# Attention scores in two passes over stacked rows, with transfers within SBUF that double q and place k's low part

## The chip, the cores and the metric

The kernel runs on one core of a Trainium2 chip. The metric is the device time in microseconds (us) of one execution. Before the change the median of 3 runs is 690.74 us (690.21 to 692.38).

The engines are called by the names of the profile: PE is TensorE (matmuls), PEld its weight loads, DVE is VectorE, ACT is ScalarE, POOL is GpSimd, SP is SyncE, which only issues transfers.

## The reference

The input x holds 8 x 512 = 4096 tokens of 256 floats. Everything is float32.

```
xn = layernorm(x)
q, k, v = xn Wq^T, xn Wk^T, xn Wv^T            # 16 heads of 16 features
qf, kf = [1, q/2, (q x q)/(4 sqrt 2)], same of k   # so qf.kf = 1 + s/4 + s^2/32,  s = q.k
A = tril(qf kf^T);  y = A v;  z = 1 / (sum over the lower row of A + 1e-12)
attn = (y z) Wo^T
ffn  = top-2 of 8 experts by xn Wg, weights by softmax: (silu(xn W1) * (xn W2)) W3
out  = x + attn + ffn
```

Since 2(1 + s/4 + s^2/32) = (1 + s/4)^2 + 1, the kernel needs only s = q.k of every head, one square per element and a sum.

## The kernel before

The program has an attention phase (up to about 329 us) and an expert phase (71 tiles of 128 rows, to the end). The change touches the attention phase alone.

**Batches and quads.** The outer unit is a batch b of 512 tokens (8 of them); a batch has 4 quads of four heads each, n = 4b + qd, 32 quads in all. k and q are laid out so that a group g (two quads) fills the 128 partitions: partition 32r + 16h + c is feature c of head r in quad 2g + h. One step "c" makes one such array of 128 x 512 in PSUM: ("c", b, 0) is q of group 0, ("c", b, 1) is k of group 0, ("c", b, 2) and ("c", b, 3) are q and k of group 1.

**High and low parts.** A float32 product is made of fp32r matmuls of a high part and a low part. ACT writes the high part (a copy to fp32r), DVE the rest (a subtraction). For q these are `Qh` and `Ql` (128 x 512 each). For k they are `Kh` and `Kl`, and each is written twice, once with the rows of h = 0 alone and once with those of h = 1 (the mask `km` zeroes the other rows), so that a matmul over 32 partitions takes one head's 16 features and 16 zeros.

**The scores.** `scores(n, part)` makes s for four heads at once, four matmuls of 32 partitions side by side (r = 0 to 3). Part 0 has 512 columns, part 1 has 384, part 2 has 256 twice. Each is made of three passes: Kh with Qh, Kh with Ql, Kl with Qh. After each part ACT squares it into T (lines 503, 511 and 517), POOL masks its diagonal (451), and `attend` multiplies by v a quad later (1026). A part's PSUM banks are free for the next part when ACT has squared it.

**Order.** PE's queue in a quad is: scores part 0, attend of the quad before, scores part 1, the steps of `slot_b`, scores part 2, the steps of `slot_c`. The steps fill PE's time while ACT squares. Steps are "x" (transpose of the normalised tokens, L1037), "c" (L1046), "v" (L1055), "C" and "T" (prefix sums of v), "t" (transpose of the attention result, L1075, then the division on DVE, lines 704 to 710), "y" (L1081), "o" (output projection, L1090), "r" (routing). Each takes one of three PSUM banks in turn and has to wait until DVE has released the step three places earlier (`free`). ACT and DVE run their own part of each step in the same order; every engine works its queue strictly in order.

**SP's queue** is one list in program order: loads of x, loads of expert weights into space that the attention phase does not use, and stores of finished rows of `out`. A transfer that waits holds up all behind it.

## Time and profile before

| | us |
|---|---|
| median of 3 runs | 690.74 |
| the profiled execution | 691.0 |
| its span | 689.3 |
| PE busy | 656.5 (95%) |
| DVE busy | 411.7 (60%) |
| ACT busy | 337.8 (49%) |
| POOL busy | 347.0 (50%) |

The span is what the profiler saw on the core; 1.7 us of the execution lie around it. A time that is given as a point, such as 169.94, counts from the start of the span. Matmuls are pipelined, so that rows of PE overlap: how long a piece of PE's work takes is read from start to start. A row can have in brackets how long its engine was idle before it, and which instruction ended that. DMA transfers show two durations: the time of the issuing instruction on its queue (SPq, ACTq), and the time from issue to landing.

### The profile page before, as it was taken

The page shows a single profiled execution, that of the slowest core. Times are in us where ns is not written, and L with a number is a line of the kernel's source. Part 1 is how long each engine was busy: PE and PEld are TensorE (multiplying, and loading weights), DVE is VectorE, ACT ScalarE, POOL GpSimd, SP SyncE. Part 2 cuts the span into 40 slices and gives each one's busy share as a digit, 9 for nine tenths or more (in the row PEclk, how much of TensorE's full clock was granted, in tenths as well). Part 3 has the DMA queues.
Part 4 walks back from the last instruction along what each step waited for, and adds up shares of the span by engine and source line. Part 5 has one row for each costly group of instructions (what it writes and reads, how often), then busy time and mean ns, then how long its engine had stood idle before and what let it go on. Part 6 is the DMA issues. An engine that isn't in the chain of part 4 may idle for free.

```text
span 689.3 us, 17082 instructions
## 1 busy us (share of the span) xinstructions
PE 656.5 (95%) x5863; PEld 511.5 (74%) x5863; DVE 411.7 (60%) x1086; ACT 337.8 (49%) x531; POOL 347.0 (50%) x381
## 2 busy tenths in 40 slices
PE   8899999999999999987899999999999999999994
PEld 6566676666766666653788888888888888888884
DVE  6866776777767666577796544444454545454442
ACT  3667767777768575665573232323232332323231
POOL 3264554546463634456065554545555555545442
PEclk9999999999999999999999999999999999999998
DMA  5220141322211121332853333333333333233332
GB/s 186 76 79 21 49 141 41 101 82 70 67 61 60 58 72 49 110 111 68 298 140 62 64 50 63 53 59 56 56 58 55 61 52 64 49 62 51 64 44 27
DMA packets 29583, 51.50 MB, mean 75 GB/s; under 512 B 4192, under 2 KB 21728, under 8 KB 29504
## 3 DMA queue, kind: packets, MB, share of 16 engines
q0 software_dynamic: 16704, 28.12, 20.7%
q1 hardware_dynamic: 12368, 21.77, 9.7%
q8 instruction: 53, 0.87, 0.5%
q10 hardware_dynamic: 432, 0.53, 0.2%
q14 instruction: 26, 0.21, 0.1%
HBM read 27.72 MB, written 22.68 MB: 73 GB/s over the span
## 4 chain that ended last, share of the span: by engine, by line
PE 85%; DVE 7%; ACT 3%; issue 2%; DMA 1%; POOL 0%; POOLq 0%; SPq 0%; DVEq 0%; ACTq 0%
PE banks L1146 29%; PE banks L1167 15%; PE banks L1026 10%; PE banks L1008 9%; PE banks L1046 7%; PE banks L1155 4%; PE banks L1090 4%; PE banks L1055 3%; PE banks L1135 2%; DVE Kl L724 2%; ACT Kh L533 2%; PE banks L1075 1%; DVE yw L696 1%; DMA wqk_r<-wqk 1%; PE banks L1081 1%
## 5 line engine op out<-in xcount | busy, mean ns | idle before, releaser
L478 POOL DMA_INDIRECT out<-yo,xw x71 | 112.2, 1581 | 155.0 <-DVE yo L966 140.0
L451 POOL TENSOR_SCALAR_AFFINE_SELECT T<-T 128x512 f32<-128x512 f32 x128 | 83.6, 665 | 131.3 <-ACT T L517 45.8
L602 ACT ACTIVATE sTh<-banks 128x512 fp32r<-128x512 f32 x71 | 42.5, 598 | 193.0 <-PE banks L1155 190.0
L1146 PE MATMUL banks<-w12h,xgh 128*128 x284 | 117.8, 415 | 2.3 <-DVE xa L753 1.7
L958 DVE TENSOR_TENSOR sTl<-banks,sTh 128x512 fp32r<-128x512 f32 x71 | 49.1, 691 | 118.2 <-ACT sTh L602 118.2
L1146 PE MATMUL banks<-w12l,xgh 128*128 x284 | 112.1, 395 | 0.0
L1146 PE MATMUL banks<-w12h,xgl 128*128 x284 | 112.1, 395 | 0.0
L467 POOL DMA_INDIRECT xg<-xs_scr,glist x71 | 73.2, 1031 | 22.7 <-issue 19.3
L1026 PE MATMUL banks<-T,vau 128*17 128x512 f32 (+3 forms) x1024 | 77.2, 442 | 0.8 <-POOL T L451 0.8
L503 ACT ACTIVATE T<-banks 128x1024 f32<-128x1024 f32 x64 | 62.1, 1026 | 28.1 <-PE banks L1008 28.0
L442 POOL DMA_INDIRECT xs_scr<-xb,slots x64 | 63.6, 994 | 16.0 <-issue 9.5
L511 ACT ACTIVATE T<-banks 128x768 f32<-128x768 f32 x64 | 48.5, 810 | 34.3 <-PE banks L1008 29.6
L517 ACT ACTIVATE T<-banks 128x768 f32<-128x768 f32 x64 | 48.5, 809 | 28.5 <-PE banks L1008 28.5
L1146 PEld LDWEIGHTS banks<-w12h,xgl 128*128 128x128 f32 x284 | 53.3, 188 | 12.0
L1008 PE MATMUL banks<-Qh,Kh 32*128 32x256 f32 (+2 forms) x512 | 57.1, 397 | 5.4 <-ACT T L517 4.7
L1026 PEld LDWEIGHTS banks<-T,vau 128*17 128x17 f32 x1024 | 26.5, 98 | 47.2 <-issue 39.9
L1146 PEld LDWEIGHTS banks<-w12h,xgh 128*128 128x128 f32 x284 | 53.8, 189 | 9.4 <-issue 2.7
L1146 PEld LDWEIGHTS banks<-w12l,xgh 128*128 128x128 f32 x284 | 53.9, 190 | 6.2
L966 DVE TENSOR_SCALAR yo<-banks,xw 128x256 f32<-128x256 f32 x71 | 34.3, 484 | 39.3 <-PE banks L1167 31.8
L979 DVE TENSOR_TENSOR hs<-banks,hs 128x512 f32<-128x512 f32 x71 | 49.1, 692 | 10.2 <-PE banks L1146 0.8
L1167 PE MATMUL banks<-w3h,sTh 128*128 x284 | 51.1, 302 | 0.8 <-ACT sTh L602 0.8
L1008 PEld LDWEIGHTS banks<-Qh,Kh 32*128 32x128 f32 x512 | 28.1, 182 | 29.6 <-ACT T L503 13.5
(179 smaller groups left out, 1354.3 us busy)
## 6 DMA issues: line engine op xcount, KB each, us to landing
w12r<-w SPq DMA_DIRECT2D x16, 512.0 KB, 4.4
out<-xa SPq DMA_DIRECT2D x16, 256.0 KB
w3r<-w SPq DMA_DIRECT2D x8, 512.0 KB, 5.2
xa<-x SPq DMA_DIRECT2D x7, 512.0 KB, 4.3
xg<-xs_scr,glist POOLq DMA_INDIRECT x71
out<-yo,xw POOLq DMA_INDIRECT x71
xs_scr<-xb,slots POOLq DMA_INDIRECT x64
wqk_r<-wqk SPq DMA_DIRECT2D x1, 512.0 KB, 6.2
```

Of the source, the lines that this page charges most:

```text
L442: e.indirect_dma_start(xs_d, bass.IndirectOffsetOnAxis(slots[:, k, 4 * b + blk:4 * b + blk + 1].bitcast(U32), 0), xb[b % 2][:, blk, :], No ...
L451: e.affine_select(out=v, in_=v, pattern=[[0, 4], [1, P]], compare_op=ALU.is_ge, fill=-1.0, base=0, channel_multiplier=-1).then_inc(s["g_mk ...
L467: e.indirect_dma_start(xg[:, t % GR, :], None, xs_d, bass.IndirectOffsetOnAxis(glist[:, t:t + 1].bitcast(U32), 0)).then_inc(s[f"d_g{t % GR ...
L478: e.indirect_dma_start(out, bass.IndirectOffsetOnAxis(xw[:, t % 4, NE:NE + 1].bitcast(U32), 0), yo[:, t % 2, :], None, compute_op=ALU.add) ...
L503: e.activation(T0[n % 2][:, 2 * h:2 * h + 2, :], banks[:, 2 * h:2 * h + 2, :], ACT.Square, scale=0.25, bias=1.0).then_inc(s["a_s"], 1)
L511: e.activation(T1[:, 2 * h:2 * h + 2, :], banks[:, 2 * h:2 * h + 2, 0:384], ACT.Square, scale=0.25, bias=1.0).then_inc(s["a_s"], 1)
L958: e.tensor_tensor(sTl[:], banks[:, 5, :], sTh[:].bitcast(F32), ALU.subtract).then_inc(s["v_st"], 1)
L979: e.tensor_tensor(hs[:], banks[:, 2 * (t % 2) + 1, :], hs[:], ALU.mult).then_inc(s["v_mu"], 1)
L1008: i = e.matmul(banks[:, r, c0:c0 + w], k[rr, jm * P:(jm + 1) * P], q[rr, 512 - w:512], start=(p == 0), stop=(p == 2))
L1026: i = e.matmul(banks[32 * r:32 * r + HA, 4, 512 - w:512], vau[b % 2][:, jm, 4 * qd + r, :], v[:, r, :], start=(jm == 0), stop=(jm == 2), s ...
L1146: i = e.matmul(banks[:, 2 * (t % 2) + m, :], a[:, k, :], w[:, bass.ds(expert[t] * 4 + (2 * k + m), 1), :], start=(k == 0 and n == 0), stop ...
L1167: i = e.matmul(banks[:, 6 + t % 2, 0:256], a[:, k * P:(k + 1) * P], w[:, bass.ds(expert[t] * 4 + k, 1), :], start=(k == 0 and n == 0), sto ...
```

## The change

`Kh`, `Kl`, `Qh`, `Ql` and `km` go. In their place:

- `K2[:, g, h]`: for head half h, partitions of h hold k's high part and the 16 partitions beside them (of the other half) hold the low part of the same features. ACT writes the high part of all rows into both copies (h = 0 and 1) in one instruction from PSUM; DVE writes the low part of all rows into one buffer `Kt`; then `move_k` copies 16 partitions of `Kt` onto the other half's partitions of `K2`, by four transfers within SBUF (r = 0 to 3) for each h.
- `Q2[g][:, h, p]`: p = 0 is q's high part, p = 1 the low part. ACT and DVE write each for both h at once (128 x 1024 in place of 128 x 512); then `move_q` copies the 16 rows of h, both parts, onto the 16 rows beside them, again four transfers for each h.
- The scores have two passes: K2 with p = 0 and K2 with p = 1. Each sums over 32 partitions, so that (high + low) of k meets high of q, then low of q.
- PE waits for the transfers at part 0 of every quad (`d_q{g}{h}`, `d_k{g}{h}`). DVE waits before it overwrites `Kt` until the transfers from it have landed.
- k and q of group 0 of the next batch are made in `slot_c` of quad 1 and `slot_b` of quad 2 (before: `slot_b` of quads 2 and 3); both "o" steps go to quad 3. In batch 0 all four "v" steps come before the first scores.
- All moves are issued by SP, but for the very first of k, which ACT issues. There are 32 transfers a batch.

```diff
 def slot_b(n):
...
-    else:
-        steps = [("c", b + 1, 3 - qd)]
+    elif qd == 2:
+        steps = [("c", b + 1, 0)]
+    else:
+        steps = [("o", b - 1, 0)] if b else []
 def slot_c(n):
...
-    steps = [("o", b - 1, qd // 2)] if b and qd != 2 else []
     if qd == 3:
-        return steps + [("y", b, 0), ("C", b + 1, 0)]
-    return steps + [("v", b + 1, 2 * qd - 2), ("v", b + 1, 2 * qd - 1)]
+        return ([("o", b - 1, 1)] if b else []) + [("y", b, 0), ("C", b + 1, 0)]
+    return ([("c", b + 1, 1)] if qd == 1 else []) + [("v", b + 1, 2 * qd - 2), ("v", b + 1, 2 * qd - 1)]
...
-FIRST = (("x", 0, 0), ("x", 0, 1), ("c", 0, 1), ("c", 0, 0), ("v", 0, 0), ("v", 0, 1))
+FIRST = (("x", 0, 0), ("x", 0, 1), ("c", 0, 1), ("c", 0, 0), *(("v", 0, i) for i in range(4)))
...
+        def move_q(e, b, g, h):
+            done(e, "c", b, 2 * g)
+            for r in range(4):
+                to, of = 32 * r + 16 * (1 - h), 32 * r + 16 * h
+                e.dma_start(Q2[g][to:to + 16, h].bitcast(F32), Q2[g][of:of + 16, h].bitcast(F32)).then_inc(s[f"d_q{g}{h}"], 16)
+        def move_k(e, b, g, h):
+            done(e, "c", b, 2 * g + 1)
+            for r in range(4):
+                to, of = 32 * r + 16 * (1 - h), 32 * r + 16 * h
+                e.dma_start(K2[to:to + 16, g, h, :].bitcast(F32), Kt[of:of + 16, :].bitcast(F32)).then_inc(s[f"d_k{g}{h}"], 16)
...
# ACT, step "c"
-                    e.activation(Qh[k // 2][:], bank("c", b, k), ACT.Copy).then_inc(s["a_qh"], 1)
-                    for h in range(2):
-                        e.activation(Kh[:, k // 2, h, :], bank("c", b, k), ACT.Copy, scale=km[:, h:h + 1]).then_inc(s["a_kh"], 1)
+                    both = bank("c", b, k).unsqueeze(1).to_broadcast([P, 2, 512])
+                    if k % 2 == 0:
+                        e.activation(Q2[g][:, :, 0, :], both, ACT.Copy).then_inc(s["a_qh"], 1)
+                    else:
+                        e.activation(K2[:, g], both, ACT.Copy).then_inc(s["a_kh"], 1)
...
# DVE, step "c"
-                    release(e.tensor_tensor(Ql[k // 2][:], bank("c", b, k), Qh[k // 2][:].bitcast(F32), ALU.subtract), "c", b, k)
+                    release(e.tensor_tensor(Q2[g][:, :, 1, :], bank("c", b, k).unsqueeze(1).to_broadcast([P, 2, 512]),
+                                            Q2[g][:, :, 0, :].bitcast(F32), ALU.subtract), "c", b, k)
...
-                    for h in range(2):
-                        i = e.scalar_tensor_tensor(Kl[k // 2][:, h, :], bank("c", b, k), km[:, h:h + 1],
-                                                   Kh[:, k // 2, h, :].bitcast(F32), ALU.mult, ALU.subtract)
-                    release(i, "c", b, k)
+                    if 2 * b + g:
+                        for h in range(2):
+                            e.wait_ge(s[f"d_k{1 - g}{h}"], MOVES * (b + g))
+                    release(e.tensor_tensor(Kt[:], bank("c", b, k), K2[:, g, 0, :].bitcast(F32), ALU.subtract), "c", b, k)
...
# PE, scores
-                if part == 0 and h == 0:
-                    done(e, "c", b, 2 * g)
-                    done(e, "c", b, 2 * g + 1)
+                if part == 0:
+                    e.wait_ge(s[f"d_q{g}{h}"], MOVES * (b + 1))
+                    e.wait_ge(s[f"d_k{g}{h}"], MOVES * (b + 1))
...
-                    for p, (k, q) in enumerate(((Kh[:, g, h], Qh[g]), (Kh[:, g, h], Ql[g]), (Kl[g][:, h], Qh[g]))):
+                    for p in range(2):
```

PE's queue in quad 1 of a batch (from scores part 1 on), before the change. L1008 are scores, L1037 "x", L1075 "t", L1090 the output projection "o" of the batch before.

```order
L1008 MATMUL banks<-Qh0_90,Kh_72 128x384 x4
L1008 MATMUL banks<-Ql0_92,Kh_72 128x384 x4
L1008 MATMUL banks<-Qh0_90,Kl0_94 128x384 x4
L1037 MATMUL banks<-ident_49,xb1_135 128x128 x8
L1075 MATMUL banks<-ident_49,yw0_100 128x128 x4
L1008 MATMUL banks<-Qh0_90,Kh_72 128x256 x4
L1008 MATMUL banks<-Ql0_92,Kh_72 128x256 x4
L1008 MATMUL banks<-Qh0_90,Kl0_94 128x256 x4
L1008 MATMUL banks<-Qh0_90,Kh_72 128x256 x4
L1008 MATMUL banks<-Ql0_92,Kh_72 128x256 x4
L1008 MATMUL banks<-Qh0_90,Kl0_94 128x256 x4
L1090 MATMUL banks<-Woh_150,yTh_148 128x256
```

The same place in the changed kernel; L1034 are scores, L1063 "x", L1101 "t", L1072 the step "c" for k of group 0 of the next batch.

```order
L1034 MATMUL banks<-Q20_89,K2_71 128x384 x8
L1063 MATMUL banks<-ident_49,xb1_131 128x128 x8
L1101 MATMUL banks<-ident_49,yw0_95 128x128 x4
L1034 MATMUL banks<-Q20_89,K2_71 128x256 x16
L1072 MATMUL banks<-xTh_139,Wqh_141 128x512
L1072 MATMUL banks<-xTh_139,Wql_142 128x512
L1072 MATMUL banks<-xTl_140,Wqh_141 128x512
```

Twelve score matmuls of 384 columns became eight, 24 of 256 became 16, and the step behind part 2 is "c" where it was "o".

DVE's queue in quad 0 of a batch, from the copy of CT on, before the change; Ql1 is q's low part of group 1, rd and yn the division of step "t", xb1 the normalised tokens of the next batch, Kl1 k's low part.

```order
L740 COPY CT_75<-banks 128x16
L720 TENSOR_TENSOR Ql1_93<-banks,Qh1_91 128x512
L704 TENSOR_SCALAR rd_76<-banks 128x16
L706 RECIPROCAL rd_76<-rd_76 128x16
L710 TENSOR_TENSOR yn_147<-banks,rd_76 128x4x64
L674 TENSOR_SCALAR xb1_135<-xa3_133,mv_142,sm_138 128x256 x4
L724 SCALAR_TENSOR_TENSOR Kl1_95<-banks,km_52,Kh_72 128x512 x2
L749 TENSOR_TENSOR yTl_149<-banks,yTh_148 128x512
```

The same place in the changed kernel:

```order
L769 COPY CT_74<-banks 128x16
L747 TENSOR_TENSOR Q21_90<-banks,Q21_90 128x2x512
L730 TENSOR_SCALAR rd_75<-banks 128x16
L732 RECIPROCAL rd_75<-rd_75 128x16
L736 TENSOR_TENSOR yn_143<-banks,rd_75 128x4x64
L700 TENSOR_SCALAR xb1_131<-xa3_129,mv_138,sm_134 128x256 x4
L755 TENSOR_TENSOR Kt_121<-banks,K2_71 128x512
L778 TENSOR_TENSOR yTl_145<-banks,yTh_144 128x512
```

The order is the same; q's low part has twice the elements, k's low part is one instruction where it was two.

SP's queue from the load of x behind batch 1 to the stores of the batch after, before the change:

```order
L349 DMA xa_130<-x 128x4x256
L322 DMA w12r<-w 128x1024
L319 DMA out<-xa_131 128x2x256 x2
L322 DMA w12r<-w 128x1024
L349 DMA xa_131<-x 128x4x256
```

The same stretch in the changed kernel, where L307 is `move_q` and L314 `move_k`:

```order
L374 DMA xa_126<-x 128x4x256
L307 DMA Q_90<-Q_90 16x1024 x8
L314 DMA K_71<-Kt 16x512 x8
L330 DMA w12r<-w 128x1024
L314 DMA K_71<-Kt 16x512 x8
L307 DMA Q_89<-Q_89 16x1024 x8
L327 DMA out<-xa_127 128x2x256 x2
L330 DMA w12r<-w 128x1024
L374 DMA xa_127<-x 128x4x256
```

Between one load of x and the next stand 32 more transfers: q and k of group 1 of the running batch, then k and q of group 0 of the next.

## Rows read from the trace of the kernel before

**Rows 1.** The page's chain that ended last, by engine and line.

```profile
PE 85%; DVE 7%; ACT 3%; issue 2%; DMA 1%; POOL 0%; POOLq 0%; SPq 0%; DVEq 0%; ACTq 0%
```

**Rows 2.** Busy time by stretch: length, busy (instructions) of each engine, clock, DMA.

```profile
131.80:169.94 38.14, 37.05 (x468) 25.22 (x462) 28.02 (x85) 27.54 (x39) 19.75 (x26) 1.00 0.26 87
```

**Rows 3.** Timeline, PE, batch 4: start us, duration us, then what.

```profile
170.28 0.40 PE L1008 MATMUL banks<-Ql,Kh 32*128 32x512 f32 x4
170.51 0.40 PE L1008 MATMUL banks<-Qh,Kl 32*128 32x512 f32 x4
...
173.40 0.34 PE L1008 MATMUL banks<-Ql,Kh 32*128 32x384 f32 x4
173.57 0.35 PE L1008 MATMUL banks<-Qh,Kl 32*128 32x384 f32 x4
...
176.52 0.29 PE L1008 MATMUL banks<-Ql,Kh 32*128 32x256 f32 x4
176.64 0.29 PE L1008 MATMUL banks<-Qh,Kl 32*128 32x256 f32 x4
```

**Rows 4.** Timeline, quad 0 of batch 4, from step "t" to step "y".

```profile
175.41 0.60 PE L1075 MATMUL banks<-ident,yw 128*128 128x128 f32 x4
175.62 0.60 ACT L528 ACTIVATE Qh<-banks 128x512 fp32r<-128x512 f32 x1 [0.15 <-PE banks L1046]
...
176.25 0.69 DVE L720 TENSOR_TENSOR Ql<-banks,Qh 128x512 fp32r<-128x512 f32 x1 [0.92 <-ACT Qh L528]
...
177.34 0.42 DVE L710 TENSOR_TENSOR yn<-banks,rd 128x256 f32<-128x256 f32 x1
...
178.35 0.60 PE L1081 MATMUL banks<-ident,yn 128*128 128x128 f32 x4
```

**Rows 5.** Timeline, quad 1 of batch 4, the chain on DVE.

```profile
182.30 0.69 DVE L696 TENSOR_TENSOR yw<-banks,CT 128x512 f32<-128x512 f32 x1 [0.44 <-PE banks L1026]
...
185.34 1.29 DVE L717 TENSOR_TENSOR xTl<-banks,xTh 128x512 fp32r<-128x512 f32 x2
...
186.08 0.39 PE L1090 MATMUL banks<-Woh,yTh 128*128 128x256 f32 x1 [0.55 <-DVE xTl L717]
```

**Rows 6.** Timeline, quad 2 of batch 4, the high and low part of k; quad 2 of batch 3.

```profile
194.78 1.27 ACT L533 ACTIVATE Kh<-banks,km 128x512 fp32r<-128x512 f32 x2
196.08 1.41 DVE L724 SCALAR_TENSOR_TENSOR Kl<-banks,km,Kh 128x512 fp32r<-128x512 f32 x2 [2.40 <-ACT Kh L533]
...
159.41 0.39 PE L1055 MATMUL banks<-Wvh,xTh 128*128 128x264 f32 x1 [0.53 <-DVE Kl L724]
```

**Rows 7.** By line and form, 100 to 300 us: instructions of 1024 elements.

```profile
L503 ACT ACTIVATE T<-banks 128x1024 f32<-128x1024 f32 x42 | 40.8, 1027 | 17.7 <-PE banks L1008 17.7
L683 DVE TENSOR_TENSOR w12l<-w12r,w12h 128x1024 fp32r<-128x1024 f32 x6 | 7.3, 1220 | 0.1
```

**Rows 8.** Issue of single transfers on SP's queue; then landing times, by issues.

```profile
7.91 0.33 SPq L308 DMA_DIRECT2D wo_r<-wo  x1
...
301.19 0.51 SPq L322 DMA_DIRECT2D w12r<-w  x1
...
wv_r<-wv ACTq DMA_DIRECT2D x1, 264.0 KB, 6.4
...
wo_r<-wo SPq DMA_DIRECT2D x1, 256.0 KB, 2.6
```

**Rows 9.** Timeline, the start: k's high part, scores parts 0 and 1.

```profile
12.12 1.27 ACT L533 ACTIVATE Kh<-banks,km 128x512 fp32r<-128x512 f32 x2 [1.29 <-PE banks L1046]
...
15.82 0.51 PE L1008 MATMUL banks<-Qh,Kh 32*128 32x512 f32 x4
...
20.03 0.45 PE L1008 MATMUL banks<-Qh,Kh 32*128 32x384 f32 x4
```

**Rows 10.** Timeline, a wait of PE in batch 7; the stretch behind it.

```profile
311.66 0.50 PE L1008 MATMUL banks<-Qh,Kh 32*128 32x512 f32 x2 [1.77 <-ACT T L517]
...
312.00:316.00 4.00, 3.80 (x28) 1.20 (x30) 3.77 (x5) 2.25 (x3) 3.38 (x3) 0.68 0.00 0
```

More of the change, by code:

```diff
@@ L41, in slot_a @@
 def slot_a(n):
[L43 removed]
+    return [("C", 0, 0)] if n == 0 else []
 def slot_b(n):
@@ L194, in build @@
         rg = [w3_hi(2 * g, 2 * g + 2) for g in range(2)]
[L195 to L197 removed]
+        Q2 = [rg[g].take(f"Q2{g}", 2048, F32R, (2, 2, 512)) for g in range(2)]
         T0 = [w3_lo(2 * u, 2 * u + 2).take(f"T0{u}", 2048, F32, (4, 512)) for u in range(2)]
@@ L325, in load_w3 @@
                 e.dma_start(W3r[:, rows(n), :], w3[:, rows(n), :]).then_inc(s[f"d_t{n}"], 16)
+            move_q(e, 0, 0, 0)
+            move_k(e, 0, 0, 1)
+            move_q(e, 0, 0, 1)
+            for b in (2, 3):
+                e.dma_start(xa[b][:], xin[b]).then_inc(s[f"d_x{b}"], 16)
+            e.wait_ge(s["c_z"], 2)
+            e.dma_start(xs_d[SPARE:SPARE + P, :], zero[:]).then_inc(s["d_z"], 16)
+            e.dma_start(out[NTOK:NTOK + P, :], zero[:, 0:D]).then_inc(s["d_z"], 16)
             for b in range(NBATCH):
+                for h in range(2):
+                    move_q(e, b, 1, h)
+                for h in range(2):
+                    move_k(e, b, 1, h)
                 if b == 0:
@@ L334, in sync_program @@
                     load_w12(11)
+                if b < LAST:
+                    for h in range(2):
+                        move_k(e, b + 1, 0, h)
+                    for h in range(2):
+                        move_q(e, b + 1, 0, h)
                 if b:
```

39 lines of the change are left out of this document (15 added, 24 removed).

## The prediction

> **What bounds the kernel now.** I read the chain of waits first: PE stands in 85% of it, DVE in 7%, ACT in 3% [rows 1]. So the time is PE's queue, read start to start, plus the few places at which PE waits for another engine. The busy time by stretch says how much room there is: one batch takes 38.14 us, of which PE is busy 37.05, DVE 28.02, ACT 27.54 and POOL 19.75, at a granted clock of 1.00, which is the level of 2.4 GHz [rows 2]. PE thus waits about 1.1 us a batch, and the reader is to see in the timeline that this is two waits: 0.55 us in quad 1, behind DVE's xTl, and 0.53 us in quad 2, behind DVE's Kl [rows 5, 6]. Everything else in a batch is PE's own work, with DVE and ACT close behind it. That decides how I count: what PE saves is worth its whole time only where the next thing that PE needs was made with slack to spare.
>
> **What goes from PE.** One of three passes. From the second pass to the third of the same part takes 170.51 - 170.28 = 0.23 us at 512 columns, 173.57 - 173.40 = 0.17 at 384 and 176.64 - 176.52 = 0.12 at 256 [rows 3]. A quad has one part of 512, one of 384 and two jobs of 256: 0.23 + 0.17 + 2 x 0.12 = 0.64 us. Over 32 quads that is 20.5 us, and it is the most that this edit can give. The passes that stay have the same partitions and columns as before, so I give them their old length. The steps that change places are of one length: "c" is six matmuls of 512 columns, 6 x 0.23 = 1.4 us, and "o" twelve of 256, 12 x 0.12 = 1.4 us. The move itself costs PE nothing.
>
> **What is added on ACT and DVE.** ACT's q copy goes from 0.60 us [rows 4] to 1024 elements, for which an ACT row says 1.03 [rows 7]: +0.43. DVE's low part of q goes from 0.69 [rows 4] to 1024 elements, 1.22 [rows 7]: +0.53. For k, ACT goes from 1.27 for two copies [rows 6] to one of 1024, 1.03: -0.24; DVE from 1.41 for two to one of 512 elements, 0.69: -0.72. Reading a bank twice through a broadcast is shown by no row; I take the length of a plain instruction with as many elements. Its ends are 0.69 (nothing for the second copy) and 2 x 0.69 = 1.38. Sums per batch hardly change (ACT +0.4, DVE -0.4). What matters is which of them PE waits for.
>
> **Quad 0 of a batch.** Take the start of "t" on PE (175.41) as zero [rows 4]. Before, ACT's q copy starts at 0.2, Ql at 0.84, the division that follows it on DVE ends at 1.93 + 0.42 = 2.35, and "y", which needs it, starts at 2.94. There is 0.59 us of slack. Now the division is late by 0.43 + 0.53 = 0.96 and "y" wants to start 0.24 earlier (part 2 is shorter). The wait is 0.96 + 0.24 - 0.59 = 0.61 us. Quad 0 keeps 0.64 - 0.61 = 0.03 us.
>
> **Quad 1.** From the end of attend DVE runs a fixed chain: copy of yw at 182.30, routing, xTl at 185.34, and PE's step behind part 2 starts at 186.08 after 0.55 us of idle [rows 5]. The step is now "c" in place of "o", but it takes the same bank, released by the same xTl. What PE saves between attend and this point (0.17 + 0.24) only makes the wait longer, 0.96 in place of 0.55. Quad 1 keeps 0.23.
>
> **Quad 2.** PE's second "v" waits 0.53 us for Kl [rows 6]. In its place comes q's chain: 1.03 + 1.22 = 2.25 us where Kh and Kl took 1.27 + 1.41 = 2.68. It starts when ACT has squared part 1, which moves with PE. So this point moves 0.43 us relative to part 1 (PE alone would have been ready 0.24 + 0.53 sooner), and the quad keeps 0.23 + 0.17 + 0.43 = 0.83.
>
> **Quad 3.** No k or q is made in it; the rows show no wait here, and the two "o" steps need only banks long released: 0.64. Sum of a batch: 0.03 + 0.23 + 0.83 + 0.64 = 1.73 us of the 2.56 that PE saves. The rest turns into waits for DVE.
>
> **The transfers.** This is the part that no row shows. SP issues 16 in a row in quad 0 and 1 (q, then k of group 1). Single issues on SP take 0.33 to 0.51 us; landing from issue takes 2.6 us for the smallest load on SP and up to 6.4 us for the slowest row [rows 8]. I take 0.43 and 2.6. The tightest waiter is DVE, which must not write `Kt` for k of the next batch until those of this one have landed. On the old time scale, with the gains above: Q2's low part ends near 177.5, so 16 issues end at 177.5 + 6.9 = 184.4 and the last lands at 187.0. `Kt` is wanted behind "c" of quad 1: 186.08 - 0.20 + 1.45 for the step, 1.1 for ACT's copy, 188.4. That leaves 1.4 us. With the largest issue, 0.51, it is 188.3: just in time. With 6.4 us of landing it is 2.4 us late, but there DVE has some 2 us of other work before PE needs anything of it again, so the first 2 us cost little. PE's own waits (`d_q`, `d_k`) have more room: k of group 1, first half, lands by about 186 and is needed near 189; group 0 has all of quad 3. Cost taken: nothing, hidden by that room; its ends are nothing and, with every transfer at the slow row, about 0.5 us a batch.
>
> The Trainium skill, "SBUF — State Buffer", section "Door 1: The DMA port swizzle", says that a transfer's rate depends on how many of 16 ports its partitions reach, in clusters of four partitions. By it, 16 partitions reach 4 ports, an estimate of 435/16 x 4 = 109 GB/s, so 64 KB of q would take 0.6 us against an issue of 0.43. By that rule the last k transfer lands some 1.4 us later and eats the room just worked out, without a cost; no row here has so narrow a transfer.
>
> **The start.** In batch 0 the transfers are in the open. ACT: k copy from 12.12 to 13.15 [rows 9], q copy to 14.2, DVE's low part to 15.5; SP issues four (1.7 us), and the last, issued at about 16.8, lands at 19.4. Part 0 of the scores starts then and not at 15.82. Part 1 stood at 20.03 [rows 9], because "v" steps and "C" came between; the "v" steps now fill the wait, and part 1 has to wait for ACT's two squares only: 19.4 + 0.67 + 2.05 = 22.1, 2.1 us later. The shorter parts 1 and 2 give back 0.4. Start: +1.5 to +1.7; I take 1.5. The other three quads of batch 0 save 1.7 as in every batch. If the gap lets PE's clock fall to 1.2 GHz, about 1 us more: after a wait of 1.77 us in batch 7 the granted clock of the next 4 us is 0.68, a mix of the two levels [rows 10].
>
> **Batch 7.** It has little to fill PE, which then waits for ACT's squares (1.77 us in one place [rows 10]). Those follow from the scores, so a shorter pass moves them too: 3 x 0.64, and 0.03 for its quad 0: 2.0. The expert phase is not touched.
>
> **Sum.** +1.5 - 1.7 (batch 0) - 6 x 1.73 = 10.4 (batches 1 to 6) - 2.0 (batch 7) = -12.6 us. The profiled execution took 691.0: 678.4. The median of the runs, 690.74, lies 0.3 below it: 678.
>
> **Rivals.**
> - *The whole saving arrives.* DVE's longer q part finds slack (a broadcast read that is cheaper, the end at 0.69), so that quads 0 and 2 have no wait. For: DVE and ACT are busy under 75% of a batch [rows 2]. Against: the 0.59 us of slack in quad 0 and the chain in quad 1, which no edit shortens. With only the chain of quad 1 left: 7 x (2.56 - 0.41) + 2.6 (batch 7) - 1.5 = 16.1; with all of it 20.5 - 1.5 = 19. Time 672 to 675.
> - *Slower: SP's queue gates DVE.* If a narrow transfer takes SP c us to issue and L to land, `Kt` is written at 177.5 + 16c + L at the earliest, against 188.4 + 2 that DVE can absorb. At c = 0.43, L may be 6.0. At c = 0.9 and L = 2.6 it is 194.5, 4.1 us late, 7 times: 29 us against 12.6 gained, 707. It loses more than the change gains (1.8 us a batch) from c of about 0.76 on, half again the largest row of SP. For: no row of this size, no transfer within SBUF. Against: the issue of 256 KB takes 0.33 and that of 512 KB 0.51 [rows 8], so a small one should not take more.
> - *Half of it.* ACT in quad 0 (q copy, squares, k copy, "y", squares without a gap) and DVE's later `Kt` and "v" work push further waits of 0.5 to 1 us into two quads of each batch: 7 us less, 685 or so. For: both engines' gaps in quads 0 and 1 are under 1 us once stretches shrink.
> - *The new order does not carry its part* (the moved steps bring a bank wait of their own of 1.7 us or more a batch): within 2 us of 691.
>
> **Chances.** Forecast (674 to 682) 0.52; whole saving 0.18; half of it 0.17; no gain 0.05; slower 0.08. A run of this kernel can tell 0.3% (2 us) from no change. Faster by over 0.3%: 0.87; within 0.3%: 0.04; slower: 0.09. The range 671 to 687 leaves out the last two cases and the ends of the others.
>
> **What would show it right or wrong.** In the profile after: score passes start to start 0.23, 0.17 and 0.12 as before, two of each; DVE's low part of q 1.22 and ACT's copy 1.03; a batch of 36.4 us. PE idle before "y" of quad 0 by 0.6, before "c" of quad 1 by 1.0, before the second "v" of quad 2 by about 0.2 to 0.6, and none before scores part 0 behind a DMA, but for the first. The first scores at about 19.4. I am wrong if scores or `Kt` wait for DMA in every batch, if issues on SP take over 0.7 us, or if quad 0 has no wait before "y".

## The result and the profile after

The changed kernel took 687.07 us, the median of its 19 runs (683.07 to 690.13), against 690.74 us before (688.42 to 693.58, measured beside it). The medians lie 3.7 us apart, the means (686.5 and 691.2) 4.7. The ratio over all runs is 0.9929, with a 95% interval of 0.9916 to 0.9942. So it is faster, by 0.5 to 0.7%. The forecast was 678.0 with a range of 671 to 687: the direction is right, but only about a third of the 12.7 us arrived, and the time lies just outside the range. The profiled execution of the changed kernel is the slowest of the 19, 690.1 us with a span of 688.4, against 691.0 and 689.3 before. Part of what follows is that execution's own, and I say where.

The way to read such a pair is to take the same landmarks on PE in both traces and subtract. Landmarks here are the first matmul of part 0 of the scores of a quad, the first matmul of the experts, and the first transpose of `hs` of the first and the last tile.

| stretch on PE | before, us | after, us | change | forecast |
|---|---|---|---|---|
| 0 to quad 1 | 26.50 | 29.83 | +3.3 | +1.5 |
| quads 1 to 3 of batch 0 | 28.40 | 26.64 | -1.8 | -1.7 |
| batches 1 to 4 | 153.21 | 150.97 | -2.2 | -6.9 |
| batches 5 and 6 | 76.27 | 73.43 | -2.8 | -3.5 |
| batch 7 to the first expert matmul | 44.38 | 42.91 | -1.5 | -2.0 |
| from there to the first tile's transposes | 9.26 | 10.95 | +1.7 | 0 |
| to the last tile's transposes | 339.76 | 342.08 | +2.3 | 0 |
| rest of the span | 11.5 | 11.6 | +0.1 | 0 |

The last column adds up to the forecast of -12.6, the one before it to -0.9. Attention alone is 5.0 us shorter at its end; the experts hand 4.1 of that back.

The chain that ended last, by engine (answers to [rows 1]):

```profile
PE 72%; DVE 11%; issue 5%; DMA 5%; ACT 3%; SPq 2%; POOL 1%; POOLq 0%; DVEq 0%
```

PE fell from 85% to 72% of it. Busy time by stretch, batch 4 and batch 6 (columns as in [rows 2]):

```profile
169.78:207.44 37.66, 34.75 (x405) 22.53 (x400) 28.51 (x83) 28.27 (x37) 19.80 (x27) 1.00 0.46 115
244.15:280.87 36.72, 34.54 (x404) 22.52 (x398) 22.42 (x69) 26.37 (x35) 17.91 (x26) 1.00 0.44 107
```

PE's busy time dropped from 37.05 to 34.75, which is 2.3 of the 2.56 us that the pass was worth. The length of a batch dropped by 0.5 in the first row and by 1.4 in the second. The rest is idle time of PE: 2.9 and 2.2 us a batch, where [rows 2] had 1.1. To see where it stands, cut a batch into its quads. Batch 5 before, four quads (length, then PE's busy time first):

```profile
208.11:217.15 9.04, 9.04 (x112) 5.97 (x107) 6.81 (x20) 6.56 (x11) 3.82 (x6) 1.00 0.32 104
217.15:227.34 10.19, 9.63 (x121) 6.91 (x118) 8.35 (x24) 7.14 (x11) 5.15 (x9) 1.00 0.05 16
227.34:236.63 9.29, 8.76 (x103) 5.68 (x103) 5.27 (x19) 6.19 (x8) 4.65 (x6) 1.00 0.21 75
236.63:246.23 9.60, 9.60 (x139) 6.65 (x138) 6.37 (x23) 5.75 (x9) 5.47 (x7) 1.00 0.13 47
```

The same batch after, and ahead of it quad 3 of batch 4:

```profile
197.59:207.44 9.85, 9.10 (x130) 6.29 (x130) 8.47 (x25) 5.78 (x8) 6.80 (x9) 1.00 0.54 125
207.44:216.62 9.18, 8.58 (x98) 5.29 (x92) 6.84 (x18) 7.43 (x12) 3.70 (x6) 1.00 0.38 109
216.62:226.78 10.16, 8.93 (x98) 5.87 (x94) 7.12 (x22) 7.47 (x10) 4.28 (x8) 1.00 0.44 88
226.78:235.23 8.45, 8.11 (x88) 5.08 (x87) 5.99 (x21) 5.99 (x7) 5.03 (x7) 1.00 0.28 82
235.23:244.15 8.92, 8.92 (x130) 6.29 (x130) 5.87 (x23) 5.47 (x7) 6.06 (x9) 1.00 0.60 136
```

Quad 0 is longer than before by 0.14 and quad 1 as long as before, although PE works 0.5 and 0.7 us less in them. Quad 2 gains 0.84, quad 3 gains 0.68. And quad 3 of batch 4 is 0.93 longer than that of batch 5.

The two waits that were forecast are there. Quad 0 of batch 4 (answers to [rows 4]; time, duration, then what):

```profile
174.84 0.60 PE L1101 MATMUL banks<-ident,yw 128*128 128x128 f32 x4
175.04 1.03 ACT L556 ACTIVATE Q<-banks 128x1024 fp32r<-128x1024 f32 x1
176.10 1.23 DVE L747 TENSOR_TENSOR Q<-banks,Q 128x1024 fp32r<-128x1024 f32 x1 [1.17 <-ACT Q L556]
177.72 0.42 DVE L736 TENSOR_TENSOR yn<-banks,rd 128x256 f32<-128x256 f32 x1
...
178.29 0.63 PE L1107 MATMUL banks<-ident,yn 128*128 128x128 f32 x4 [0.59 <-DVE yn L736]
```

ACT's copy takes 1.03, DVE's part 1.23, and PE stands 0.59 us ahead of "y". These are the three numbers of the forecast, within 0.02. But from the start of "t" to the start of "y" it takes 178.29 - 174.84 = 3.45 us. The forecast had 2.94 + 0.96 - 0.59 = 3.31: it let "y" start when yn ends (177.72 + 0.42 = 178.14), and PE starts it 0.15 us later. Quad 1 (answers to [rows 5]):

```profile
182.04 0.69 DVE L722 TENSOR_TENSOR yw<-banks,CT 128x512 f32<-128x512 f32 x1 [0.98 <-PE banks L1052]
...
184.22 0.63 POOL L476 TENSOR_SCALAR_AFFINE_SELECT T<-T 128x512 f32<-128x512 f32 x1 [1.78 <-ACT T L536]
184.30 0.60 DVE L825 TENSOR_TENSOR eq<-oh,rk 128x32 f32<-128x32 f32 x1
...
185.36 1.29 DVE L743 TENSOR_TENSOR xTl<-banks,xTh 128x512 fp32r<-128x512 f32 x2
...
186.10 0.50 PE L1072 MATMUL banks<-xTh,Wqh 128*128 128x512 f32 x1 [1.18 <-DVE xTl L743]
```

From the copy of yw to xTl DVE needs 3.32 us here and 3.04 in [rows 5], so PE waits 1.18 and not 0.96. In between, one small instruction of DVE with two inputs in SBUF starts 0.08 us behind a mask of POOL and takes 0.60 us; before, it took 0.19 and started ahead of the mask.

What was not forecast stands in quad 3 of batch 4 (DVE's and POOL's rows of quads 2 and 3):

```profile
197.25 1.21 POOL L476 TENSOR_SCALAR_AFFINE_SELECT T<-T 128x512 f32<-128x512 f32 x2
197.36 2.18 DVE L709 TENSOR_TENSOR w12l<-w12r,w12h 128x1024 fp32r<-128x1024 f32 x1
...
202.69 0.69 DVE L722 TENSOR_TENSOR yw<-banks,CT 128x512 f32<-128x512 f32 x1
...
203.53 0.63 PE L1101 MATMUL banks<-ident,yw 128*128 128x128 f32 x4 [0.75 <-DVE yw L722]
```

DVE's split of an expert weight takes 2.18 us, and 1.22 on average before [rows 7]. It starts 0.11 us behind a pair of POOL's masks. Before, it started first, and then POOL paid (1.85 us for a pair that takes 1.21 here):

```profile
198.23 1.22 DVE L683 TENSOR_TENSOR w12l<-w12r,w12h 128x1024 fp32r<-128x1024 f32 x1
198.69 1.85 POOL L451 TENSOR_SCALAR_AFFINE_SELECT T<-T 128x512 f32<-128x512 f32 x2 [0.98 <-ACT T L517]
```

So in these rows whichever of the two starts first runs at its own length and the other waits for it. The Trainium skill, "SBUF — State Buffer", section "SBUF: two separate sides", says so of such a pair: a DVE instruction with two SBUF inputs and a GpSimd one that reads SBUF take an exclusive lock. The rows agree: the one that came second lost 0.96 us (DVE) or 0.64 us (POOL).

The transfers (answers to [rows 8]; issue min/median/max in ns, then landing, then who waited):

```profile
L307 SPq DMA_DIRECT2D Q<-Q x128: 507/589/1843, 15.9 to 292.8; - x128
...
DMA to landing us min/median/max: 2.2/2.4/3.6
...
L314 SPq DMA_DIRECT2D K<-Kt x124: 507/589/1669, 18.7 to 297.8; - x124
...
  DVE Kt L755: 17.5, 7
```

An issue costs 0.59 us in the median, not 0.43, though it moves 32 or 64 KB; landing is 2.4 for those of q. DVE waits for Kt's release seven times, 2.5 us on the average.

The start (answers to [rows 9]), and then the granted clock of three stretches (length, busy times, third from last the clock):

```profile
15.95 2.73 SPq L307 DMA_DIRECT2D Q<-Q  x4
20.55 1.23 PE L1034 MATMUL banks<-Q,K 32*128 32x512 f32 x8 [2.91 <-DMA Q<-Q]
```

```profile
20.00:28.00 8.00, 7.17 (x71) 4.64 (x71) 5.28 (x22) 4.21 (x7) 2.31 (x3) 0.57 0.45 75
300.00:312.00 12.00, 10.47 (x117) 5.28 (x109) 10.80 (x26) 6.27 (x8) 9.00 (x11) 0.86 0.54 185
320.00:328.00 8.00, 6.67 (x25) 5.36 (x26) 3.54 (x8) 3.19 (x5) 2.84 (x3) 0.57 0.75 260
```

PE is at 1.2 GHz in three places: for about 7, 3 and 7 us (a granted clock of 0.57 over 8 us means (1 - 0.57) x 2 x 8 = 6.9 us at half clock, and so on). The kernel before had one such place, of about 3 us, between 313 and 317 us, the one that [rows 10] shows in part.

Last, the scatter of the experts' results, on POOL and in DVE's copy that waits for it:

```profile
341.38 1.63 POOL L503 DMA_INDIRECT out<-yo,xw  x1 [17.35 <-DVE yo L992]
348.94 2.08 POOL L503 DMA_INDIRECT out<-yo,xw  x1 [3.62 <-DMA out<-yo,xw]
...
354.34 0.17 DVE L980 COPY xw<-xg 128x16 f32<-128x16 f32 x1 [1.74 <-DMA out<-yo,xw]
```

Each scatter waits until the one before it has landed. The first took 6.8 us to land, beside the last loads of weights, and the tiles from the sixth to the twelfth came late, together by 2.3 us. This is the +2.3 of the table. I take it for this execution's own: in eleven of the twelve traces below the same stretch takes 339.7 to 340.0 us, as before, and it is longer only with twice as many transfers (341.0), where the first scatter took 7.4 us to land. Without it the profiled execution would be 3.2 us faster than before, which fits the 3.7 of the medians.

### The profile page after: what moved, and what is told of

It is laid out like the page before. It is cut to its first block, busy times and chain, and to the rows that moved or that the text cites. A ratio compares the mean times of both kernels' runs of the same rounds, so it can differ in the third digit from the quotient of the medians.

```text
span 688.4 us, 16296 instructions
## 1 busy us (share of the span) xinstructions
PE 643.7 (94%) x5351; PEld 494.4 (72%) x5351; DVE 411.1 (60%) x1067; ACT 342.6 (50%) x515; POOL 346.5 (50%) x381
## 3 DMA queue, kind: packets, MB, share of 16 engines
q1 hardware_dynamic: 20432, 34.24, 20.3%
## 4 chain that ended last, share of the span: by engine, by line
PE 72%; DVE 11%; issue 5%; DMA 5%; ACT 3%; SPq 2%; POOL 1%; POOLq 0%; DVEq 0%
PE banks L1172 27%; PE banks L1193 14%; PE banks L1052 8%; PE banks L1034 5%; PE banks L1072 4%; PE banks L1181 4%; PE banks L1116 3%; DVE Q L747 3%; DMA out<-yo,xw 2%; PE banks L1161 2%; ACT Q L556 2%; PE banks L1081 2%; DVE yw L722 1%; PE banks L1107 1%; SPq L307 1%
## 5 line engine op out<-in xcount | busy, mean ns | idle before, releaser
L503 POOL DMA_INDIRECT out<-yo,xw x71 | 114.1, 1607 | 159.3 <-DVE yo L992 85.7
L476 POOL TENSOR_SCALAR_AFFINE_SELECT T<-T 128x512 f32<-128x512 f32 x128 | 79.8, 635 | 121.1 <-ACT T L528 51.7
L492 POOL DMA_INDIRECT xg<-xs_scr,glist x71 | 71.1, 1001 | 24.2 <-issue 23.0
L1034 PE MATMUL banks<-Q,K 32*128 32x256 f32 (+2 forms) x1024 | 71.7, 363 | 5.9 <-DMA Q<-Q 2.9
L467 POOL DMA_INDIRECT xs_scr<-xb,slots x64 | 67.2, 1050 | 18.4 <-issue 9.6
L1034 PEld LDWEIGHTS banks<-Q,K 32*128 32x128 f32 x1024 | 38.6, 185 | 30.2 <-ACT T L528 13.9
```

Source lines behind the costliest of these rows:

```text
L467: e.indirect_dma_start(xs_d, bass.IndirectOffsetOnAxis(slots[:, k, 4 * b + blk:4 * b + blk + 1].bitcast(U32), 0), xb[b % 2][:, blk, :], No ...
L476: e.affine_select(out=v, in_=v, pattern=[[0, 4], [1, P]], compare_op=ALU.is_ge, fill=-1.0, base=0, channel_multiplier=-1).then_inc(s["g_mk ...
L492: e.indirect_dma_start(xg[:, t % GR, :], None, xs_d, bass.IndirectOffsetOnAxis(glist[:, t:t + 1].bitcast(U32), 0)).then_inc(s[f"d_g{t % GR ...
L503: e.indirect_dma_start(out, bass.IndirectOffsetOnAxis(xw[:, t % 4, NE:NE + 1].bitcast(U32), 0), yo[:, t % 2, :], None, compute_op=ALU.add) ...
L1034: i = e.matmul(banks[:, r, c0:c0 + w], K2[rr, g, h, jm * P:(jm + 1) * P], Q2[g][rr, h, p, 512 - w:512], start=(p == 0), stop=(p == 1))
```

## The experiments

Each was run beside the kernel before on the same chip (its medians 691.6 to 692.2 us there). A ratio is against it. The changed kernel itself stands at 0.9929. Ratios of single edits have intervals about 0.004 wide, so they seldom tell such an edit from the changed kernel; the traces do, though each shows one execution. Where an edit is not shown, or is shown in part, "..." marks it or the text says so.

**Without the transfers.** It leaves out the copies within SBUF and the waits for them, so one of the two row halves holds the wrong part of q or k.

```diff
-            done(e, "c", b, 2 * g)
+            return
             for r in range(4):
...
# the same in move_k; DVE's wait for d_k goes; PE, scores
-                    e.wait_ge(s[f"d_q{g}{h}"], MOVES * (b + 1))
-                    e.wait_ge(s[f"d_k{g}{h}"], MOVES * (b + 1))
+                    done(e, "c", b, 2 * g)
+                    done(e, "c", b, 2 * g + 1)
```

> Leaves out the transfers within SBUF and the waits for them: the rows of q and k beside each other then both hold the high copy or the low part as written, so the result is not attention's; every instruction of PE, ACT and DVE stays. Theory A (the transfers cost only the gap at the start; what the batches lack lies on DVE and POOL): first scores near 17 instead of 20.55, quad 1 starts at about 26.5 instead of 29.83, batches 1 to 4 stay at 37.6 us and batches 5 and 6 at 36.7; the expert phase takes back a part, so 683.5 to 685.5 us against 687.1 of the changed kernel. Rival B (the issues of 0.59 us on SP and the late gate on Kt are what the batches lack): batches 1 to 6 at 36.4 as forecast, another 5 to 6 us, so 678 to 680.

Measured: 688.1 us, ratio 0.9950 (0.9931 to 0.9969). First scores at 17.64, but batch 1 starts at 57.21, later than the 56.47 with transfers. Without the gap ahead of the first scores PE waits 2.2 us for DVE's CT and 1.4 for ACT's squares between 25 and 29 us, and the clock is halved from 27 to 34. Batches 1 to 6 take 38.03, 37.68, 37.66, 37.66, 36.72 and 36.71 us, equal to the changed kernel's within 0.03.

So in a steady batch 32 transfers cost nothing. Of theory A the batches are right. The forecast of 683.5 to 685.5 failed: quad 1 starts at 28.87 and not at 26.5, because the waits come back behind the first scores, and the slow stretch comes all the same.

**The new order alone**, three passes and no transfers, the tables of slots taken from the changed kernel.

```diff
+    elif qd == 2:
+        steps = [("c", b + 1, 0)]
     else:
-        steps = [("c", b + 1, 3 - qd)]
+        steps = [("o", b - 1, 0)] if b else []
...
```

> The kernel before with three passes and no transfers, but with the new order of the steps (v steps ahead of the first scores, c in quad 2 and 1, o in quad 3). Theory A (the moved steps cost PE nothing): 690.7 within 1 us, batches of 38.1 us. Rival B (the new order brings waits of its own, above all DVE's later work in quads 2 and 3): batches of 38.6 us or more, 693 to 696 us, which would account for most of what the whole change lacks.

Measured: 689.25 us, ratio 0.9968 (0.9955 to 0.9981), batches 2 to 6 of 37.24 to 37.27. Both theories failed. Its batch 5 by quads:

```profile
206.23:215.28 9.05, 9.05 (x114) 5.98 (x108) 6.72 (x20) 6.42 (x11) 2.92 (x5) 1.00 0.35 104
215.28:225.41 10.13, 9.57 (x114) 6.59 (x110) 7.20 (x22) 8.41 (x13) 5.07 (x9) 1.00 0.05 16
225.41:233.91 8.50, 8.50 (x103) 5.63 (x102) 6.48 (x22) 5.56 (x7) 4.65 (x6) 1.00 0.14 50
233.91:243.48 9.57, 9.57 (x145) 6.90 (x145) 6.17 (x22) 5.47 (x7) 6.40 (x10) 1.00 0.22 74
```

The order alone brings nearly the whole gain of quad 2, 0.79 of 0.84 us. From these rows to the changed kernel's, the missing pass with all that comes with it (longer q parts, transfers) changes quads 0 to 3 by +0.13, +0.03, -0.05 and -0.65: it pays only in quad 3, the one quad in which PE waits for nobody. What two passes would bring in the old order with the transfers left out was not run, so the two shares hold for this sequence of steps.

**The weight split moved.**

```diff
+                if qd == 2 and (b, qd) in W12_LOW_WITH:
+                    w12_low(W12_LOW_WITH[b, qd])      # end of before_b, no longer in after_b
```

> The changed kernel with one DVE instruction moved: w12_low of quad 2 goes ahead of the slot with c, away from POOL's pair of masks. Theory A (DVE's w12l of 1.22 us is stretched to 2.18 by POOL's masks in quad 2 of batches 1 to 4, and PE pays 0.74 us for it in quad 3): w12l back to 1.22, no wait for yw before t in quad 3, batches 1 to 4 at 36.9 instead of 37.65, 3 us at the first expert matmul, 684 to 686 us at the end since the expert phase gives some back. Rival B (the quad 3 wait comes from the length of DVE's queue, not from the overlap): wait stays 0.5 us or more, or moves to the second v of quad 2 (low part of q later by up to 1.2 us): 687 to 690.

Measured: 686.03 us, ratio 0.9920 (0.9901 to 0.9939). Batches 2 to 6 take 36.73 to 36.75 each, as theory A has it; the time is at the upper end of its 684 to 686. The moved split in the timeline:

```profile
190.78 1.22 DVE L709 TENSOR_TENSOR w12l<-w12r,w12h 128x1024 fp32r<-128x1024 f32 x1
```

and quad 3 of batch 4 by stretch, no longer with idle time of PE:

```profile
194.82:203.74 8.92, 8.92 (x129) 6.28 (x128) 6.04 (x23) 5.78 (x8) 6.24 (x9) 1.00 0.61 138
```

The overlap with POOL's masks is the cause of the 0.93 us in batches 1 to 4. The next run shows it a second time, without an edit of that place. The first expert matmul comes 2.1 us sooner than in the changed kernel: 3.7 are won in batches 1 to 4, and 1.5 lost again from batch 7 to that matmul, where this trace has half clock from 295 to 299 and from 316 to 326 us.

**PE filled ahead of the first scores.**

```diff
+            for _ in range(26):
+                e.transpose(banks[:, 0, 0:P], ident[:], ident[:])
             for n in range(NQ):
                 scores(n, 0)
```

> The changed kernel with 26 transposes into bank 0 ahead of the first scores, which keep PE busy through the wait for the first transfers; nothing that is computed changes. Theory A (the 2.9 us of idle drop the granted clock to half until 26.8 us): the clock stays at 1.0 from 20 to 27 us, quad 1 starts 1.5 to 2 us sooner (28.0 instead of 29.83), 685 to 686 us. Rival B (the clock falls whatever PE does there, or the start is set by ACT's squares and DVE): quad 1 stays at 29.8, 687 us.

Measured: 686.4 us, ratio 0.9934 (0.9912 to 0.9957). Theory A failed: quad 1 starts at 31.60 and not at 28.0. The gap of 2.9 us is 1.0 us now, but the first scores come at 21.51, since SP's first four issues took 3.77 us where they took 2.73, and the clock still falls, and stays low from about 24 to 30.5 us: behind the first scores PE waits again, for ACT's squares, 0.5 us twice.

In this trace DVE's split started ahead of the masks in quad 2 of batches 2 and 3, and behind them in batches 1 and 4:

```profile
85.24 2.18 DVE L709 TENSOR_TENSOR w12l<-w12r,w12h 128x1024 fp32r<-128x1024 f32 x1
123.05 1.22 DVE L709 TENSOR_TENSOR w12l<-w12r,w12h 128x1024 fp32r<-128x1024 f32 x1
```

Quad 3 takes 8.93 and 9.15 us in batches 2 and 3, and 9.84 to 9.86 in batches 1 and 4 as in the changed kernel (though quad 2 of batch 2 is 0.57 longer here). So the order of starts is what decides, in one and the same execution.

**PE filled in all thin stretches.**

```diff
+            spin(0, 26)
             for n in range(NQ):
+                if n > NQ - 4:
+                    e.wait_ge(s["v_yw"], n - 1)
+                    spin(4, 9)
...
+                if n == 0:
+                    e.wait_ge(s["c_b4"], 1)
+                    spin(4, 8)
...
             attend(NQ - 1)
+            e.wait_ge(s["a_s"], 6 * NQ)
+            spin(2, 8)
             step("t", LAST, 3)
+            spin(2, 6)
```

> The changed kernel with idle stretches of PE filled by transposes of a constant whose result nobody reads: 26 ahead of the first scores, 8 ahead of part 1 of quad 0, 9 ahead of the scores of quads 29, 30 and 31, 14 around the last t. Theory B (a part of the gain goes to half clock: 7 us at the start, 5 in batch 7, 7 at the first expert, against one stretch of 6 in the kernel before; each is set off by a stretch in which PE mostly waits): granted clock 1.00 in at least two of the three places, first tile's transposes 3 to 4 us sooner (331 instead of 334.7), 683 to 684.5 us. Rival (the clock falls whatever fills the gaps, as it did at the start with 26 transposes alone): the same three stretches, 687 us.

Measured: 685.19 us, ratio 0.9909 (0.9892 to 0.9926); the first tile at 330.98 where the changed kernel has 334.73. The same three stretches as above:

```profile
20.00:28.00 8.00, 6.98 (x90) 4.88 (x89) 4.95 (x26) 4.69 (x8) 2.32 (x3) 1.00 0.46 80
300.00:312.00 12.00, 10.36 (x137) 6.53 (x129) 11.35 (x25) 6.71 (x9) 9.01 (x11) 1.00 0.49 179
320.00:328.00 8.00, 7.02 (x45) 5.82 (x43) 4.72 (x10) 5.13 (x8) 1.72 (x2) 1.00 0.91 323
```

The clock is 2.4 GHz in all three, and no microsecond from 8 us to the first tiles shows half clock. PE still waits here in places, up to 1.6 us for yw in batch 7, without a fall. Batch 1 starts at 55.14 instead of 56.47, although the first scores come 1.4 us later (21.92), and from the first expert matmul to the first tile it takes 9.24 instead of 10.95, as before (9.26). Theory B holds for the clock: the slow stretches cost at least 1.3 us at the start and 1.7 at the experts. Its time, 683 to 684.5, is missed by 0.7 us; the profiled execution is the fastest of the six and the one with the highest clock.

The stretch at the experts can be read in other traces as well. It takes 9.25 us where the clock does not fall behind the first expert matmul (the gather's run below), 10.19 where it stays low for 2.9 us (26 transposes alone), 10.95 for 3.7 (the changed kernel) and 12.00 for 6.1 (the second buffer, below).

**DVE's order in quads 0, 1 and 2.**

```diff
+    if qd == 0 and n:
+        return [("T", b, 0), ("t", (n - 1) // 4, (n - 1) % 4), ("c", b, 2)]
...
-                    place_rows(b)      # before_b, quad 1
...
+                elif qd == 1 and b < LAST:
+                    place_rows(b)      # after_b
```

(and the moved weight split of above)

> The changed kernel with three orders changed, nothing added: in quad 0 the step T and t go ahead of c; in quad 1 DVE makes xTl ahead of the slots of the routing; in quad 2 w12_low goes ahead of DVE's part of q. Theory A (the passes removed in quads 0 and 1 turn into waits for DVE, 0.60 before y and 1.18 before c, and are to be had once DVE's order gives them): quad 0 8.6 instead of 9.17, quad 1 9.4 instead of 10.19, batches of 35.4 us instead of 37.65 and 36.71, 12 us less at the first expert matmul, 675 to 678 us. Rival (DVE or ACT has no room, the waits reappear a quad later): batches 36.5 or more, 685 us.

Measured: 681.51 us, ratio 0.9853 (0.9831 to 0.9874); batches 37.82, 36.79, 37.01, 36.59, 35.71, 37.25. The time misses theory A's 675 to 678. Quads 0 and 1 came out nearly as it says, 8.67 and 9.52; but in five of six batches quad 2 takes 9.5 to 10.2. DVE's row behind quad 1 of batch 4:

```profile
187.70 0.69 DVE L757 TENSOR_TENSOR Kt<-banks,K 128x512 fp32r<-128x512 f32 x1 [3.02 <-DMA K<-Kt]
```

and quad 2 by stretch, PE idle for 1.1 us of it:

```profile
185.37:194.84 9.47, 8.41 (x88) 4.91 (x87) 7.04 (x22) 7.36 (x9) 8.70 (x10) 1.00 0.34 97
```

Here the rival is right as well: a wait comes back a quad later. Its candidate is Kt's release, which now comes 3 us late.

**The gather behind the masks.**

```diff
-                    if n == NQ - 1 and m == 1:
+                    if n == NQ - 1 and m == 3:
```

> The changed kernel with POOL's first gather behind the last two masks instead of ahead of them. Theory C (the gather waits 2.7 us for the last rows sent, and the masks behind it hold PE for 2.1 us at the end of attention): attend of quad 31 waits under 0.6 us, the gather itself starts no later (316.6), the first expert matmul 1.5 to 2 us sooner (322 instead of 323.8); at the end 1 to 2 us less, 685 to 686. Rival (the landing of the gather sets the first expert): attend is sooner, but the expert's first matmul stays at 323.8 and the time at 687.

Measured: 685.25 us, ratio 0.9908 (0.9884 to 0.9932), which overlaps the changed kernel's. From quad 31's first scores to the first expert matmul it takes 15.0 us; the changed kernel takes 18.1 and the kernel before 17.1. In the changed kernel PE's waits of that stretch are led by this one (us in total, times, longest):

```profile
PE banks L1052 <- POOL T L476: 2.3, 2, 2.1
```

It is gone here, and the clock does not fall at the experts. The gather starts at 318.26, which is 10.6 us after quad 31's start, where it was 10.9. Of theory C the wait holds. Its size is less sure: with the gather in its old place the stretch also takes only 16.4 us in the run with 26 transposes and 16.7 in that with a second buffer, so that 1.4 to 3.1 us are the gather's. And the first expert matmul is at 322.75 and not at 322, since quad 31 itself starts 2.0 us later here, behind half clock from 300 to 303 us.

**The old order with two passes and transfers.** The tables of slots are those of the kernel before.

> The changed kernel (two passes, transfers) with the order of steps of the kernel before. In it DVE's low part of q for the next quad 0 ends about 2 us before that quad's first scores, and 4 issues and a landing of some 2.4 us come behind it. Theory A (the new order is what hides the transfers, and brings 0.9 us a batch by itself): PE waits 2 to 4 us for a transfer ahead of the scores of quad 0 in every batch, batches of 39 to 41 us, 700 to 715 us. Rival (the transfers find room in either order): batches of 37.5 to 38, 687 to 690 us.

Measured: 718.97 us, ratio 1.0397 (1.0366 to 1.0429); batches of 40.8 to 42.6. Theory A's mechanism holds, its 700 to 715 us are too low. PE's waits in one batch of it (146.88 to 187.67):

```profile
PE banks L1033 <- DMA Q<-Q: 5.5, 2, 2.8
```

So the new order is what hides the transfers. "Made a quad sooner" is no extra of the change but its condition: without it, the kernel would have been 27 us slower than before.

**A second buffer for Kt.**

```diff
-                    if 2 * b + g:
+                    if b:
                         for h in range(2):
-                            e.wait_ge(s[f"d_k{1 - g}{h}"], MOVES * (b + g))
+                            e.wait_ge(s[f"d_k{g}{h}"], MOVES * b)
...
# and Kts[g] in the place of Kt
```

> The changed kernel with a second buffer for Kt, one per group, so that DVE need not wait until k's transfers of group 1 have landed. Theory A (DVE waits 2.5 us for that in every batch, but PE needs nothing of DVE in that time): the wait on DVE goes, batches stay at 37.66 and 36.72 us, time 687 within 1 us. Rival B (SP's queue gates DVE and through it PE): batches of 36.4 or less, 678 to 681 us.

Measured: 687.0 us, ratio 0.9931 (0.9906 to 0.9955); batches 38.01, 37.67, 37.65, 37.66, 36.71, 36.74. DVE's wait for the transfers is gone and PE gains nothing.

**Both: the three orders and the second buffer.** It has the edits of the last run and of the one with three orders.

> The run with the three changed orders, and the second buffer for Kt as well. Theory A (with quads 0 and 1 shortened the room in front of Kt is used up: DVE waits 2.9 us for the transfers, and quad 2 then takes 9.6 to 10.2 us instead of 8.45): quad 2 back to 8.6 to 9.0, batches of 35.5 us instead of 36.6, 7 us less: 674 to 676 us against 681.5. Rival (quad 2's length there comes from DVE's moved w12_low and the slots of the routing): batches of 36.5 us, 681.

Measured: 679.62 us, ratio 0.9814 (0.9797 to 0.9830). Batches are 35.64 to 35.70 from batch 2 on; quad 2 of batch 5:

```profile
219.57:228.10 8.53, 8.19 (x87) 4.98 (x86) 5.85 (x21) 5.99 (x7) 7.76 (x10) 1.00 0.39 111
```

That settles quad 2 above: it was Kt's release. A buffer that is worth nothing in the changed kernel is worth 1 us a batch once PE is faster. The first expert matmul is at 315.62, but the clock is halved for 10 us at the start and for twice 7 us around the end of attention, and the time is 4 us above theory A's 674 to 676. How much of these 4 us is the clock's was not run by itself.

**Everything that showed a gain**: the three orders, the second buffer, the later gather and the filled stretches, and in the expert phase the copy of xw moved behind the weight splits.

> All edits that showed something: the three changed orders, the second buffer for Kt, the gather behind the masks, the filled idle stretches of PE, and in the expert phase DVE's copy of xw and its wait for the scatter moved behind the splits of the weights. Theory A (they are independent: orders and buffer 12 to 13 us, clock 2, gather 1 to 2): 670 to 673 us, clock above 0.99. Rival (they share the same gain, since the expert phase starts sooner than its weights land): 675 to 678 us.

Measured: 675.34 us, ratio 0.9761 (0.9746 to 0.9776), clock 0.993. It is the fastest version here, 2.4% below the kernel before and 1.7% below the changed one. It misses 670 to 673: its first expert matmul is at 311.56, but the first tile needs 10.14 us from there, not 9.25. ACT waits for the first load of W3:

```profile
316.81 1.06 ACT L586 ACTIVATE w3h<-w3r 128x1024 fp32r<-128x1024 f32 x1 [2.97 <-DMA w3r<-w]
```

and PE stands idle for 2.5 us behind it. The loads of W3 are what is late next, as the rival had it with its 675 to 678 us.

**Twice as many transfers of half the size.**

```diff
-                e.dma_start(K2[to:to + 16, g, h, :]..., Kt[of:of + 16, :]...)
+                for c in (slice(0, 256), slice(256, 512)):
+                    e.dma_start(K2[to:to + 16, g, h, c]..., Kt[of:of + 16, c]...)
...
# in move_q one transfer for each of p = 0 and 1; MOVES = 128
```

> The changed kernel with each transfer cut into two of half the columns: twice as many issues, the same bytes. Theory A (an issue on SP costs about 0.6 us whatever the size): 16 issues ahead of Kt's release take 19 us instead of 9.5, Kt is written some 9 us later, and since its slack is used up by the 2.5 us that DVE already waits, 7 to 9 us a batch are lost: 735 to 750 us. Rival (an issue costs by its bytes, so two halves cost as much as one): 687 to 692 us.

Measured: 796.9 us, ratio 1.151 (1.148 to 1.154), batches of about 50 us. Two bursts on SP's queue, 16 issues each:

```profile
159.81 10.42 SPq L316 DMA_DIRECT2D K<-Kt  x16
170.28 10.86 SPq L308 DMA_DIRECT2D Q<-Q  x16
```

An issue of 16 KB takes 0.65 us in such a burst and one of 32 KB 0.68; the median of the changed kernel, with 32 and 64 KB, is 0.59. Theory A's mechanism holds, its size is too small: besides Kt (DVE waits up to 13.2 us) the q transfers now come late for PE too (up to 4.8 us ahead of the scores).

## Why the forecast was wrong, step by step

The gap between the forecast of -12.6 and the profiled execution without the late scatter (-3.2) is 9.4 us. The steps that failed, with what each is worth:

- **"Quad 3: No k or q is made in it; the rows show no wait here ... 0.64": failed in batches 1 to 4.** It is the largest single piece: (1.42 x 4) - 2.24 = 3.4 us, where 1.42 is what batches 5 and 6 gained each and 2.24 what batches 1 to 4 gained together. I looked at which engine PE waits for, not at what changes place beside what. A shift of half a microsecond between DVE and POOL turned "DVE first" into "POOL first", and PE then waits 0.75 us for yw. The run with the moved split shows it, and so do the two batches of the run with 26 transposes.
- **"Quad 1 keeps 0.23" and "quad 0 keeps 0.64 - 0.61 = 0.03": mis-sized.** They kept 0.03 and -0.14, while quad 2 kept 0.84 for a forecast of 0.83. The waits before "y" and "c" are where the forecast had them, of 0.59 us for 0.61 and 1.18 for 0.96. In quad 0 the sum left out the 0.15 us from the end of yn to the start of "y". In quad 1 DVE's chain is 0.28 longer than before. The instruction beside POOL's mask is 0.41 longer than before and a later one 0.13 shorter, which makes the 0.28, but I did not run this by itself. With quad 3 at 0.68 the batch keeps 1.42 where I had 1.73: 0.31 x 6 = 1.9 us.
- **"The move itself costs PE nothing": right in cost, wrong in what it left out.** The new order alone is worth 0.88 us a batch, and the pass with all that comes with it 0.54. I gave quad 2's gain to a shorter chain of q against k, 2.25 against 2.68 us. The run with the order alone has three passes and q's short parts, and gains nearly the same in quad 2, so the gain belongs to the order. That quad 2's forecast of 0.83 met 0.84 is therefore in part luck.
- **"The transfers": they cost nothing in a batch, as forecast, on a wrong price.** Issue 0.59 and not 0.43, the gate 2.5 us late and not 1.4 early; DVE absorbed it, as the text said of "some 2 us of other work". The run without transfers and the one with two buffers show zero. The rival "SP's queue gates DVE" had its break-even at about 0.76 us an issue; doubling their number shows the cliff.
- **"The start": mis-sized, +3.3 for +1.5.** The first scores came at 20.55 and not at 19.4, since q's low part was done 0.4 us later and SP took 2.73 us for four issues where I had 1.7. From there to quad 1 it took 9.28 us where the forecast had 8.6, at half clock from 20.3 to 27.1. In the run with filled stretches, at full clock, it took 7.35. So the clock, which I named and did not count ("about 1 us more"), cost up to 1.9 us there, and the rest of that sum was 1.2 us too high.
- **"Batch 7": -1.5 for -2.0**, with a half-clock stretch of 3 us in it.
- **"The expert phase is not touched": failed**, by 1.7 us in this trace. PE waits 2.1 us for masks behind a gather that waits for its rows, then for yw and yn; the clock falls at 320 us, and the first expert begins at half clock. The kernel before had its slow stretch earlier, at 313 to 317, and so none here. In the run with filled stretches this 1.7 is gone.

Of the rivals, "half of it" (685 or so) came nearest to the time and to the mechanism, further waits of 0.5 to 1 us; but it had one in two quads of each batch, and the runs show one in quad 3 of four batches. Most of what is missing beyond the batches is clock and the price of the first issues. What makes the clock fall in one place and not in another stays open: the runs show where it fell and what it cost.
